# A third buffer for routed rows, the edges' places put by ScalarE, and a shorter inverse root in a fused GNN kernel

## The reference

```python
x = _layernorm(x + _L0_gnn_ref(x, edge_index, 6250), axis=-1)
x = _layernorm(x + _L1_gnn_ref(x, edge_index, edge_attr_40, edge_weight, node_type_119, node_vec, ...), axis=-1)
# layer 0: out[dst] += x[src] * deg_inv_sqrt[src] * deg_inv_sqrt[dst]
# layer 1:
gate = silu(edge_attr @ W1.T + b1) @ W2.T + b2 + sum(emb[z[src]] * (emb[z[dst]] @ adaptW.T))
cw = where(distances < 6, 0.5 * (cos(pi * distances / 6) + 1), 0)
mj = node_mult[dst]
msg = gate * h[dst] * (cw * mj)[:, None]
agg = segment_sum(msg, src) / clip(segment_sum(mj, src), 1e-8)
x = (h + agg, normalized over channels) * gamma + beta
```

## Time and profile before

| | |
|---|---|
| median of 3 runs | 2958.45 us (2950.31 to 2959.36) |
| the profiled execution | 2955.32 us, of which the span of the trace is 2953.5 us |
| mean granted TensorE clock | 0.838 of full speed |
| busy | VectorE 82%, TensorE 76%, GpSimd 69%, ScalarE 49% |

### The profile page before, as it was taken

One profiled execution on the slowest core, in us unless ns is written; L12 is line 12 of the kernel. 1 busy time (PEld: TensorE's weight loads), 2 busy tenths in 40 slices (PEclk: granted clock), 3 DMA queues, 4 the chain that ended last, 5 costly groups with the idle time before them and its releaser, 6 DMA issues.

```text
span 2953.5 us, 73730 instructions
## 1 busy us (share of the span) xinstructions
PE 2258.0 (76%) x25909; PEld 1950.9 (66%) x25909; DVE 2431.3 (82%) x5426; ACT 1436.9 (49%) x3029; POOL 2034.2 (69%) x1852
## 2 busy tenths in 40 slices
PE   6980477888777787777777888788888888888675
PEld 5770366667566676666666677777777777777675
DVE  9994488778787787878888788888888888888798
ACT  7983244545454454544544444444444454545123
POOL 7505777777777777777777777777777777750255
PEclk9765689888888888988998888888888888889897
DMA  8405334444434444434455555444454544452895
GB/s 314 167 0 151 78 102 120 127 118 127 118 115 124 123 119 125 119 116 122 134 149 148 150 149 150 147 146 149 148 148 146 148 147 148 147 148 100 358 391 210
DMA packets 167528, 439.21 MB, mean 149 GB/s; under 512 B 85302, under 2 KB 85302, under 8 KB 147446
## 3 DMA queue, kind: packets, MB, share of 16 engines
q1 hardware_dynamic: 96266, 233.49, 23.7%
q0 software_dynamic: 67888, 194.98, 22.8%
q10 hardware_dynamic: 3004, 5.90, 0.6%
HBM read 291.23 MB, written 142.99 MB: 147 GB/s over the span
## 4 chain that ended last, share of the span: by engine, by line
POOL 36%; issue 18%; PE 17%; DVE 12%; DMA 6%; ACT 2%; DVEq 0%; POOLq 0%; ACTq 0%; SPq 0%
POOL slot L719 34%; DMA erows<-slots 5%; PE acc L1607 4%; PE route L816 4%; PE pwin L772 3%; DVE oh_r L1095 3%; POOL slots L727 2%; PE gate L754 2%; DVE eoh L1184 1%; PE pwin L837 1%; PE phid L742 1%; DVE val L1215 1%; DVE val L1212 1%; ACT routed L889 1%; DVE val L1219 1%
## 5 line engine op out<-in xcount | busy, mean ns | idle before, releaser
L719 POOL DMA_INDIRECT slot<-table,gidx x1616 | 1733.6, 1073 | 610.9 <-issue 610.0
L816 PEld LDWEIGHTS route<-parts,oh_r 128*128 128x128 bf16 x11312 | 780.1, 101 | 95.4 <-issue 70.0
L816 PE MATMUL route<-parts,oh_r 128*128 128x148 bf16 x11312 | 827.1, 234 | 3.4 <-DVE parts L1235 3.1
L1095 DVE TENSOR_SCALAR oh_r<-iota_r,spot 128x896 bf16<-128x896 f16 x1616 | 651.0, 463 | 78.7 <-PE route L816 67.3
L889 ACT ACTIVATE routed<-route 128x444 bf16<-128x444 f32 (+1 forms) x1010 | 508.7, 514 | 271.0 <-PE route L816 260.7
L772 PEld LDWEIGHTS pwin<-win,oh_t 128*128 128x128 bf16 x4848 | 283.7, 124 | 241.3 <-ACT ssum L899 127.1
L772 PE MATMUL pwin<-win,oh_t 128*128 128x80 bf16 (+1 forms) x4848 | 298.7, 237 | 137.5 <-ACT ssum L899 134.8
L851 PE MATMUL pwin<-slot,oh_d 128*128 128x144 bf16 x1616 | 146.6, 254 | 259.5 <-DMA slot<-table,gidx 228.6
L851 PEld LDWEIGHTS pwin<-slot,oh_d 128*128 128x128 bf16 x1616 | 135.9, 150 | 273.1 <-issue 149.9
L742 PE MATMUL phid<-attr,w 80*96 80x512 f32 x404 | 265.3, 744 | 48.5 <-issue 39.5
L754 PE MATMUL gate<-w,hid 97*128 97x96 f32 x1616 | 268.6, 319 | 2.0 <-ACT hid L877 1.9
(11 more groups left out here) (228 smaller groups left out, 3297.1 us busy)
## 6 DMA issues: line engine op xcount, KB each, us to landing
rows<-slots SPq DMA_DIRECT2D x51, 1295.0 KB, 8.7
oh_t<-dst_row SPq DMA_DIRECT2D x101, 512.0 KB
erows<-slots SPq DMA_DIRECT2D x51, 777.0 KB
attr<-in_edge_attr SPq DMA_DIRECT2D x101, 320.0 KB
slots<-zeros SPq DMA_DIRECT2D x53, 518.0 KB
slot<-table,gidx POOLq DMA_INDIRECT x1616
table<-tab SPq DMA_DIRECT2D x3, 676.0 KB, 5.5
weight_t<-weights SPq DMA_DIRECT2D x101, 8.0 KB
```

What stands on the lines that cost most here:

```text
L719: e.indirect_dma_start(out=slot[:, s % (U // 2), g, :], out_offset=None, in_=table0, in_offset=bass.IndirectOffsetOnAxis(ap=gidx[:, s, g:g ...
L816: mm = e.matmul(route[:, (NPH * m + phase) % 2, RC * (j - a):RC * (j - a + 1)], oh_r[:, c, slot_of, :], parts[:, s % 2, c, :], start=(c == ...
L1095: oh = e.tensor_scalar(oh_r[:, c], iota_r[:, :, :], spot[:, s % 2, c:c + 1], None, ALU.is_equal)
```

## The change

Three things, of which two move work in the pass over the tiles.

1. `routed` has three buffers (`RB`). The scatters raise three semaphores in turn, and every wait that counted pairs of tiles now counts threes. The first copy of tile t waits for the scatter of tile t - 3.
2. VectorE's step `keys` is gone. ScalarE copies the places within `put_got(0)`, between the copy of the features and that of the factors. `split_ok` counts two for each tile.
3. In `normalize` the halving, the shift and the subtraction become two instructions with two operations each beside the addition of epsilon, which nothing waits for any more.

A semaphore `ones_ok` at the start is also dropped.

```diff
+RB = 3
...
-            routed = sb("routed", [P, 2, ROW], BF16, ph)
+            routed = sb("routed", [P, RB, ROW], BF16, ph)
...
                     e.indirect_dma_start(out=perm, out_offset=bass.IndirectOffsetOnAxis(
-                        ap=sidx[:, s:s + 1], axis=0), in_=routed[:, s % 2, :], in_offset=None
-                        ).then_inc(scattered[s % 2], 16)
+                        ap=sidx[:, s:s + 1], axis=0), in_=routed[:, s % RB, :], in_offset=None
+                        ).then_inc(scattered[s % RB], 16)
...
-                        if m == 0 and since(i, s, 2):
-                            e.wait_ge(scattered[s % 2], 16 * pair_of(i, s))
+                        if m == 0 and since(i, s, RB):
+                            e.wait_ge(scattered[s % RB], 16 * (U // RB * i + s // RB))
...
                         if since(i, s, 2):
                             e.wait_ge(routing, 2 * NPH * (U * i + s - 1))
+                        if m == 0:
+                            e.activation(parts[:, s % 2, :, RC - 1], key16[:, bass.ds((U * i + s) * G, G)], ACT.Copy)
                         of_mult = parts[:, s % 2, m * HC:(m + 1) * HC, 0:3 * MW].rearrange(
                             "p (b k) (j c) -> p b k j c", b=2, c=MW)[:, :, :, :, C]
                         e.activation(of_mult, by_bank[:, :, :, WX:WW], ACT.Copy).then_inc(got_ok, 1)
...
-                    done(e.tensor_scalar(ve, mv[:, 1:2], EPS, None, ALU.add))
-                    done(e.tensor_scalar(nh, ve, -0.5, None, ALU.mult))
-                    done(e.tensor_scalar(c.bitcast(I32), ve.bitcast(I32), 1, None, ALU.logical_shift_right))
-                    done(e.tensor_scalar(root.bitcast(I32), c.bitcast(I32), -1.0, float(MAGIC), ALU.mult, ALU.add))
+                    e.tensor_scalar(ve, mv[:, 1:2], EPS, None, ALU.add)
+                    done(e.tensor_scalar(nh, mv[:, 1:2], EPS, -0.5, ALU.add, ALU.mult))
+                    done(e.tensor_scalar(root.bitcast(I32), ve.bitcast(I32), -0.5, float(MAGIC), ALU.mult, ALU.add))
...
-                def keys(i, s):
-                    t = U * i + s
-                    if since(i, s, 2):
-                        wait_apart(e, routing, 2 * NPH * (t - 1), passed)
-                    if not since(i, s, 1):
-                        e.wait_ge(weights_out, 16)
-                    e.tensor_copy(parts[:, s % 2, :, RC - 1], key16[:, bass.ds(t * G, G)]).then_inc(split_ok, 1)
```

More of the change, by code:

```diff
@@ L566, in build @@
         x1 = base
-        scattered = [sem(f"scattered{s}") for s in range(2)]
+        scattered = [sem(f"scattered{s}") for s in range(RB)]
         weights_out = sem("weights_out")
@@ L618, in tile_programs @@
              hidden, hid_sb, ranked, placed, routing, rows_ok, picked, got_ok, gated, own, gate_used,
-             val_ok, high, rested, mid, split_ok, stepped, group_rows, ones_ok) = (
+             val_ok, high, rested, mid, split_ok, stepped, group_rows) = (
                 sem(n) for n in ("sx", "ohd", "ohb", "oht", "ohr", "summed_f", "taken", "halved", "chain",
@@ L623, in tile_programs @@
                                      "got_ok", "gated", "own", "gate_used", "val_ok", "high", "rested_f",
-                                     "mid", "split_ok", "stepped", "group_rows", "ones_ok"))
+                                     "mid", "split_ok", "stepped", "group_rows"))
             erows_in, ecopied, emade, esummed, emb_kept = (
@@ L697, in early_rows @@
                     if isinstance(v, int) and v == 0:
-                        for par in range(2):
-                            e.wait_ge(scattered[par], 16 * ((EARLY_FROM - 3 - par) // 2 + 1))
+                        for k in range(RB):
+                            e.wait_ge(scattered[k], 16 * ((EARLY_FROM - 3 - k) // RB + 1))
                     else:
@@ L806, in step @@
                         t = U * i + s
-                        e.wait_ge(split_ok, 3 * t + m + 2)
+                        e.wait_ge(split_ok, 2 * t + m + 1)
                         e.wait_ge(ohr, 2 * (2 * t + m + 1))
@@ L861, in tensor @@
                 with when(e, 1):
-                    e.wait_ge(ones_ok, 1)
                     e.wait_ge(a_own, W_PUT)
@@ L888, in step @@
                             e.wait_ge(routing, NPH * (2 * t + m) + phase + 1)
-                            e.activation(routed[:, s % 2, RC * (HS * m + a):RC * (HS * m + b)],
+                            e.activation(routed[:, s % RB, RC * (HS * m + a):RC * (HS * m + b)],
                                          route[:, (NPH * m + phase) % 2, 0:RC * (b - a)], ACT.Copy
@@ L1076, in put_rows @@
                     if since(i, s, U):
-                        e.wait_ge(scattered[s % 2], 16 * (pair_of(i, s) - U // 2 + 1))
+                        e.wait_ge(scattered[s % RB], 16 * (U // RB * (i - 1) + s // RB + 1))
                     e.wait_ge(group_rows, t + 1)
@@ L1091, in step @@
                         else:
-                            e.wait_ge(split_ok, 3 * t + 2)
+                            e.wait_ge(split_ok, 2 * t + 1)
                         for half in range(2):
@@ L1245, in done @@
                     e.wait_ge(v, steps[0])
-                e.memset(hid[2 * C:2 * C + 1, :], 1.0).then_inc(ones_ok, 1)
+                e.memset(hid[2 * C:2 * C + 1, :], 1.0)
                 e.wait_ge(dst_at, 16)
@@ L1272, in vector @@
                 with when(e, 1):
-                    over_tiles(e, NT, U, (spots, 5), (keys, 5), (logits(0), 5), (onehots, 0), (messages(0), 5), (normalize, 2), (steps_of_groups, 5),
+                    over_tiles(e, NT, U, (spots, 5), (logits(0), 5), (onehots, 0), (messages(0), 5), (normalize, 2), (steps_of_groups, 5),
                                (buckets, 4), (route_onehots(0), 5), (put_rows, 5),
@@ L1557, in sync @@
                 if fits:
-                    for parity in range(2):
-                        e.wait_ge(scattered[parity], 16 * ((NT - parity + 1) // 2))
+                    for k in range(RB):
+                        e.wait_ge(scattered[k], 16 * ((NT - k + RB - 1) // RB))
                     for b in range(NB):
```

## The result

The changed kernel takes 2943.2 us (median of 5 runs, 2929.77 to 2951.41) beside 2958.45 us for the kernel before (5 runs, 2946.88 to 2966.27). The ratio is 0.9946, with an interval of 0.9922 to 0.9970: 16 us faster by the ratio, 15 by the medians. I had said 2953, with a range from 2944 to 2966. The time lies just outside, on the fast side, where I had put the rival "GpSimd is freed" (2943, chance 0.07).

What follows compares the result with a forecast made beforehand. GpSimd bounds 400 to 1,613 us; until 2,655 us a circle through several engines does, with VectorE's queue late in 15 visits. 15 x (0.30 + 0.07) = 5.6 us off 2958.45 gives 2953, range 2944 to 2966.

Steps and rivals of the forecast that it cites:

- GpSimd is freed: Rival: VectorE's copy holds up gathers in GpSimd's 52 tiles; removal gains up to 9.9 us, time 2943, chance 0.07.
- Whatever VectorE or ScalarE save here is given back in a wait for the gathers: Step for 400 to 1,613 us, where GpSimd is full: savings on VectorE or ScalarE count for nothing.
- The root: Inverse root in `normalize`: 0.75 to 0.45 us, saving 0.30 us in 15 visits after 1,613 us, nothing before.
- The places on VectorE: Copy leaving VectorE's queue ahead of `normalize`: 0.07 us saved in the same 15 visits, bounds 0.07 and 0.19 us.
- The places on ScalarE: Added copy delays `got_ok` of half 0 by 0.12 to 0.31 us, hidden behind TensorE's `layer2(0)`: no cost.
- Three buffers: ScalarE's first routed copy follows its routing by 0.98 us, the scatter never late: a third buffer gains nothing.
- The branch: Rival: VectorE's 2.79 us stall behind the loop's branch shortens by 1 us in seven turns: 2946, chance 0.10.
- The loads: Rival: 26 `erows` loads on the chain (144 us, mean 5.5) grow by 0.7 us each: 2971, chance 0.13.

Runs made afterwards that it cites:

- buffers: Kernel before with only three buffers for routed rows and `ones_ok` dropped: 2955.76 us, ratio 1.0003 against the kernel before at 2955.19 us.
- root: Kernel before with only the shorter inverse root in `normalize`: 2954.20 us, ratio 1.0000 against the kernel before at 2955.19 us.
- places: Kernel before with only the copy of the edges' places moved from VectorE to ScalarE: 2942.21 us, ratio 0.9965.
- nowhere: Kernel before with the copy of the places on neither VectorE nor ScalarE, last column of `parts` zeroed once: 2940.76 us, ratio 0.9962.
- all again: The whole changed kernel repeated against the kernel before (2955.19 us): 2945.00 us, ratio 0.9966.
- all: The whole changed kernel in the first comparison with the kernel before (2958.45 us): 2943.2 us, ratio 0.9946.

## Why the prediction was wrong

**The step that failed** is "Whatever VectorE or ScalarE save here is given back in a wait for the gathers", with the dismissal of "GpSimd is freed" that hangs on it. What VectorE does sets how long the gathers take, and so the pace of the stretch that GpSimd bounds. That rival's price, up to 9.9 us and a time of 2943 us, came out right by luck: it was 52 times the copy's own 0.19 us, and no gather was held up by the copy itself. From the first scatter to the 47th, which are 46 tiles of GpSimd's own stretch, I took the times from the timelines of seven executions: with VectorE's copy 1071.9, 1081.1 and 1083.8 us (before, buffers, root), without it 1060.3, 1067.8, 1073.7 and 1076.1 us (places, nowhere, all again, all). The means are 1078.9 and 1069.5 us: some 9.5 us. From the gathers it comes out about the same: in those executions their mean length (400 to 1,580 us) falls from 1.079 to 1.065 us, and 46 tiles x 16 gathers x 0.014 us = 10.3 us. The single executions overlap (1071.9 with the copy, 1076.1 without it), so one trace of each wouldn't have shown this. The mean gather barely separates them (1,073 ns the shortest with the copy, 1,070 the longest without). What shows that the copy costs time are the ratios; that the time goes to GpSimd's gathers rests on seven traces. This is the larger part of the 10 to 16 us measured. The remainder is within what the single profiles vary by in the other stretches: from the 47th scatter to the last they take 1247.6 to 1270.3 us.

**Why the row misled me.** I read the earlier trace rows as a test: the gather over the copy took 0.94 us, so the copy holds nobody up. It couldn't have been one. What decides a gather's length is whether VectorE is in an instruction of certain kinds about 0.12 us after the gather starts (the last section has the count), and this copy began 0.19 us after. In the three traces with the copy only 3 gathers had it under way at that moment, and they took 0.97 us at most. So the copy lengthens no gather itself. But VectorE's long instructions come at a time that the short ones before them set. In 26 of 52 tiles of the trace of before (400 to 1,600 us) the product stands right behind the copy, and the copy puts it and what follows back by 0.07 us.

**A shift at work.** That such a shift is enough to lengthen a gather can be seen in the traces, at the other change on VectorE. The chain of `normalize` and the gathers beside it, before (`step_at` is the first instruction behind `normalize`):

```profile
480.93 0.15 DVE L1135 TENSOR_SCALAR small<-mv 128x1 f32<-128x1 f32 x1
...
483.44 0.94 POOL L719 DMA_INDIRECT slot<-table,gidx  x1 [0.30 <-issue]
483.58 0.28 DVE L1070 TENSOR_TENSOR step_at<-iota_f,rstart_t 52x128 f32<-52x128 f32 x1
...
484.69 1.94 POOL L719 DMA_INDIRECT slot<-table,gidx  x1 [0.30 <-issue]
486.93 1.09 POOL L719 DMA_INDIRECT slot<-table,gidx  x1 [0.30 <-issue]
```

and in the changed kernel:

```profile
484.44 0.15 DVE L1137 TENSOR_SCALAR small<-mv 128x1 f32<-128x1 f32 x1
...
486.86 0.28 DVE L1072 TENSOR_TENSOR step_at<-iota_f,rstart_t 52x128 f32<-52x128 f32 x1
486.96 2.95 POOL L720 DMA_INDIRECT slot<-table,gidx  x1 [0.30 <-issue]
487.06 0.57 DVE L1055 TENSOR_TENSOR oh_b<-number,bkt 128x816 bf16<-128x816 bf16 x1
...
490.21 1.08 POOL L720 DMA_INDIRECT slot<-table,gidx  x1 [0.30 <-issue]
```

Before, `step_at` starts 2.65 us after the first small instruction and 0.14 us after a gather, and this gather takes 0.94 us. With the shorter root it starts after 2.42 us, 0.10 us ahead of the same gather, and the gather takes 2.95 us, since `oh_b` and the one-hots `oh_r` follow without a gap. Between 400 and 1,580 us this befalls seven gathers in each of the three traces with the shorter root (2.94 or 2.95 us, once 2.25), and in the same seven tiles of the four traces without it none (0.94 or 0.95 us). Part of it is made up, as a later gather was lengthened in the old order. What all gathers of these seven tiles take beyond 0.943 us each is 13.5 us (before) and 14.3 (buffers) against 21.8 (root), and without the copy 10.3 (places) and 13.9 (nowhere) against 19.2 (all again) and 21.5 (all). That is some 8 us more with the shorter root. Over all gathers between 400 and 1,580 us it is 4 to 6 us more: 112.4 us against 105.0 and 111.4, and 101.4 and 102.6 against 93.6 and 98.1. So the root, which I had costed at nothing in this stretch, lengthens gathers there. That may be why its 4.5 us don't show in 1.0000; with so few traces it isn't shown.

For the copy's 0.07 us I can't point at such a place. By kinds of instruction, the excess over 0.943 us of the gathers that have `oh_r` beside them at 0.12 us sums to 50.6, 46.2 and 37.4 us with the copy (before, buffers, root) and to 37.6, 42.1, 33.7 and 34.9 us without (places, nowhere, all again, all). Beside `oh_d` it is 23.9, 30.0 and 32.3 against 22.3, 26.1, 25.6 and 25.6 us. The root alone has as little beside `oh_r` as the kernels without the copy, so a low sum there isn't the copy's mark by itself. The gain arises some us away from the copy, at other instructions. That the shift brings it is argued from this and not shown.

The Trainium skill's rule on the shared port (SBUF — State Buffer, "SBUF: two separate sides") was the right pointer, and I was wrong to put it aside for the sake of one gather. But its 2-port modes, which I named, aren't what the earlier trace rows shows: `oh_d` is a `tensor_tensor`. For it the same section has the other clause, an instruction with two SBUF inputs against a GpSimd instruction that reads SBUF. The traces agree that such instructions lengthen gathers; with the other lengthened gathers the excess is 93.6 to 112.4 us in each trace.

**The other steps.** *The root:* sized right in place (0.44 us for 0.45), and mis-sized as nothing before 1,613 us, as said. Its 15 x 0.30 = 4.5 us on the path were neither seen nor excluded by 1.0000 [0.9977, 1.0022]. On the Trainium skill's rule about semaphores between Vector instructions (VectorE: DVE Perf Modes, "The DRAIN you can't avoid") the trace after disagrees again: L1138 starts 0.07 us after L1137, which lasts 0.15 us. I had left out that the section itself excepts an instruction that isn't held, which starts earlier. *The places on VectorE:* 0.07 us of the queue, right (0.08). As a price of the copy it was the term that was mis-sized: 15 x 0.07 = 1.1 us, where the runs give 10 to 13 us (0.9965 and 0.9962 of 2955 and 2952 us). *The places on ScalarE:* 0.11 us (0.12 to 0.31 forecast), hidden, right. *Three buffers:* nothing, right (1.0003; the first copy is 0.99 us behind its routing). *The branch:* the six stalls of VectorE behind it in the second stretch are each 0.8 to 1.3 us or 2.5 to 3.2 us, and sum to 11.5 us before, to 7.8 us after, and to 8.1 us with the buffers alone. They vary from one execution to the next, and the change doesn't set them. *The loads:* on the chain 21 of them with 123.4 us, 5.9 us each, in place of 26 with 144 us, 5.5 each: near what I had.

## What to carry to other kernels

Where GpSimd is full with indirect DMAs, VectorE's queue isn't free even if nobody waits for VectorE: count the lengthened gathers and ask what moves against them, and let a rival that needs this have more than one row's evidence. A row that shows no direct effect of an instruction doesn't show that the kernel is the same without it. A saving on such a queue can also move a long instruction under the start of a gather and cost time, as the shorter root did. And where two single executions of a kernel differ by as much as the gain, compare several traces of each, and in them a quantity with hundreds of samples (here the mean gather) beside the spans.

## What the traces showed of the hardware

What lengthens a gather can be read instruction by instruction. GpSimd and VectorE in the kernel with the places alone (timeline; its L1050 is `oh_d`, its L1055 `oh_b`):

```profile
1053.54 0.94 POOL L719 DMA_INDIRECT slot<-table,gidx  x1 [0.30 <-issue]
1054.54 0.43 DVE L1195 TENSOR_TENSOR prod<-kept,got 128x256 f32<-128x256 f32 x1 [5.04 <-ACT parts L958]
1054.79 0.99 POOL L719 DMA_INDIRECT slot<-table,gidx  x1 [0.30 <-issue]
...
1055.34 1.22 DVE L1050 TENSOR_TENSOR oh_d<-number,w 128x2048 bf16<-128x2048 bf16 x1
1056.09 1.28 POOL L719 DMA_INDIRECT slot<-table,gidx  x1 [0.30 <-issue]
...
1058.46 0.57 DVE L1055 TENSOR_TENSOR oh_b<-number,bkt 128x816 bf16<-128x816 bf16 x1
1058.92 0.94 POOL L719 DMA_INDIRECT slot<-table,gidx  x1 [0.30 <-issue]
```

At 1053.66, 0.12 us into the first gather, VectorE was idle, and the gather took 0.94 us. The second began under the product, which ended at 1054.97, and took 0.99 us: it ended 0.81 us after the product. The third began under `oh_d` (to 1056.56) and ended at 1057.37, again 0.81 us later. The last began under `oh_b`, which ended 0.11 us into it: 0.94 us. Where VectorE's instructions follow each other without a gap the gather waits for the first gap: the one of 2.95 us above ends 0.81 us after such a gap in `oh_r`.

Over the seven traces from chips on which the kernel before takes about 2,955 us (gathers that start between 400 and 1,580 us), with VectorE in `oh_r`, `oh_d`, `oh_t`, `prod`, or one of the differences that read or write `parts`, 0.12 us after their start, 2,163 of 2,732 were lengthened by over 0.05 us. With VectorE idle then, or in a reduction, or in the sum with the gate or the product with the weights, it was 11 of 2,209. Between them stand `eoh` (37 of 38), `oh_b` (35 of 57) and the product with `got` (57 of 226). So the shape and the kind of the instruction count and not only that it runs, and what counts is one moment of the gather: `val<-gate` at 1056.47 to 1057.02 lay within the third gather, which still ended 0.81 us after `oh_d`. Why the product with the weights (f32, 128x384, both inputs in SBUF) lengthens hardly any (1 of 250) and the differences of the same shape, which read `parts`, 187 of 212, the runs don't show.
